# Four sublayers on one core: attention heads rotated in quarters inside the steady loop, and one joint block ahead of the delta rule

## Time and profile before

| | |
|---|---|
| median of 3 runs | 3130.51 us (3123.18 to 3131.16) |
| profiled execution | 3129.02 us, its span 3127.2 us |
| PE busy | 2824.0 us, 90% |
| DVE busy | 1693.7 us, 54% |
| ACT busy | 1081.3 us, 35% |
| POOL busy | 806.9 us, 26% |
| mean granted TensorE clock | 0.947 |

### The profile page before, as it was taken

How to read it: one execution, slowest core, us unless ns; L and a number is a source line. 1 busy time by engine, 2 the same in 40 slices (tenths; PEclk the granted TensorE clock), 3 DMA queues, 4 the chain that set the end, 5 groups by cost and what they waited for, 6 DMA issues and landing times. The chain is left out here.

```text
span 3127.2 us, 38699 instructions
## 1 busy us (share of the span) xinstructions
PE 2824.0 (90%) x13678; PEld 2330.6 (75%) x13678; DVE 1693.7 (54%) x2466; ACT 1081.3 (35%) x1592; POOL 806.9 (26%) x835
## 2 busy tenths in 40 slices
PE   5955888849999999999999749999999878999998
PEld 4754778748888888888888537878888657888887
DVE  4744667564554455444553556666566354465464
ACT  2332433322121111211111317777777612222221
POOL 0006767400000000000000047888878610000000
PEclk8976889969999999999999879999999999999999
DMA  2322222110010000100000030000000001001001
GB/s 81 114 72 54 56 73 57 40 48 21 20 40 20 20 20 20 40 20 20 20 21 0 26 135 24 30 29 28 27 27 28 14 27 41 27 14 40 3 25 41
DMA packets 86058, 114.35 MB, mean 37 GB/s; under 512 B 42512, under 2 KB 62992, under 8 KB 83152
## 3 DMA queue, kind: packets, MB, share of 16 engines
q1 hardware_dynamic: 85968, 113.18, 11.6%
HBM read 86.16 MB, written 26.74 MB: 36 GB/s over the span
## 5 line engine op out<-in xcount | busy, mean ns | idle before, releaser
L1845 POOL TENSOR_TENSOR att_p_lo<-att_probs,att_p_hi 128x768 fp32r<-128x768 f32 x256 | 467.0, 1836 | 120.5 <-ACT att_p_hi L1910 117.1
L1984 DVE TENSOR_REDUCE att_top<-att_q_scores 128x1 f32<-128x1024 f32 x250 | 305.8, 1223 | 223.0 <-PE att_q_scores L2072 215.8
L297 DVE TENSOR_TENSOR fp_hidden<-fp_gelu,fp_up 128x512 f32<-128x512 f32 x128 | 88.0, 688 | 447.6 <-PE fp_up L75 384.8
L1921 ACT ACTIVATE att_probs<-att_k_scores 128x1024 f32<-128x1024 f32 x256 | 262.6, 1026 | 133.9 <-PE att_k_scores L2088 129.9
L1606 POOL MEMSET lat_power<- 128x16 f32 x1 | 0.1, 111 | 1077.8 <-POOLq L52 1077.8
L286 DVE TENSOR_TENSOR k_stream<-k_stream,fp_down 128x512 f32<-128x512 f32 x256 | 175.5, 686 | 91.0 <-PE fp_down L75 87.4
L347 ACT ACTIVATE fp_gelu<-fp_gate 128x512 f32<-128x512 f32 x128 | 76.2, 595 | 421.8 <-PE fp_gate L75 420.8
L2072 PE MATMUL att_q_scores<-att_k_stack,att_q_stack 128*128 128x512 f32 x500 | 189.4, 460 | 28.3 <-DMA att_q_stack<-att_k_stack 14.4
L73 PE MATMUL fp_gate<-f_feat_hi,fp_w_hi 128*128 128x512 f32 x512 | 200.0, 391 | 13.3 <-DVE fp_w_lo L266 13.3
L1910 ACT CAST att_p_hi<-att_probs 128x768 fp32r<-128x768 f32 x256 | 211.5, 826 | 0.0
L74 PE MATMUL fp_gate<-f_feat_lo,fp_w_hi 128*128 128x512 f32 x512 | 199.8, 390 | 0.0
(11 more groups left out here) (343 smaller groups left out, 6502.5 us busy)
## 6 DMA issues: line engine op xcount, KB each, us to landing
f_words<-codes SPq DMA_DIRECT2D x16, 768.0 KB
f_scale<-scales SPq DMA_DIRECT2D x16, 768.0 KB
f_staged<-w_sparse SPq DMA_DIRECT2D x12, 1024.0 KB, 4.8
qkv<-pc_rows SPq DMA_DIRECT2D x9, 1024.0 KB, 4.4
dr_raw<-qkv SPq DMA_DIRECT2D x16, 576.0 KB, 6.2
att_q_stack<-rotated SPq DMA_DIRECT2D x64, 128.0 KB
att_k_stack<-rotated SPq DMA_DIRECT2D x64, 128.0 KB
k_stream<-hidden SPq DMA_DIRECT2D x4, 1024.0 KB, 9.0
```

The lines of the kernel that those rows point to most:

```text
L1845: pool.tensor_tensor(p_lo[:, buffer, :], probs[:, slot, 0:SPLIT], p_hi[:, buffer, :].bitcast(F32), ALU.subtract).then_inc(lo_done, 1)
L1921: act.activation(probs[:, t, :], k_scores[:], ACT.Exp).then_inc(exp_done, 1)
L1984: dve.tensor_reduce(top[buffer][:, STACK + t:STACK + t + 1], scores[:], AX.XY, ALU.max, negate=True).then_inc(max_done, 1)
```

## The change

One function, `project_front`, takes the place of the first block, `normalise`, `project_conv` and `gates_and_decays`. Latent attention prepares only `PREPARED = 2` passes in its prologue; passes 2 to 7 are prepared two passes ahead, a quarter of a pass (256 tokens of a quad) in each head of passes 0 to 5, by `project_piece`, `rotate_piece`, `high_piece`, `low_piece` and `store_piece`, in the bank `turned`. GpSimd's addition goes to VectorE. `passes` has no loop any more. The result `mixed` is written over `values`.

In `project_front`, SP issues: tokens 0, identity, gate weights, tokens 1, gate rows, tokens 2, the first three weight tiles, tokens 3, taps, masks; then the stores and loads of the convolution as before. GpSimd takes the power of four tiles at a time. The transposes and the gates have two PSUM buffers each. The orders of ScalarE, VectorE and TensorE, their helpers left out:

```diff
         @block.scalar
...
+            high(0)
+            act.wait_ge(gate_w_in, 16)
+            act.copy(gate_hi[:], gate_w[:]).then_inc(gate_hi_done, 1)
+            high(1)
+            for i in range(TILES):
+                if i + 2 < TILES:
+                    high(i + 2)
+                gate(i)
+                if i == TILES // 2:
+                    high_weights(0, 0)
+
+            act.preload_act_table_set("natural_log_exp_and_others")
...
+            act.preload_act_table(ACT.Silu)
+
             body(0, True, False)
         @block.vector
...
+            for i in range(SUB):
+                stats(i)
+            moments_of(0)
+            scale(0)
+            scale(1)
+            low(0)
+            dve.wait_ge(gate_hi_done, 1)
+            dve.tensor_tensor(gate_lo[:], gate_w[:], gate_hi[:].bitcast(F32), ALU.subtract).then_inc(gate_lo_done, 1)
+            for i in range(TILES):
+                if i + 2 < TILES:
+                    scale(i + 2)
+                if i:
+                    low(i)
+                if i < 2:
+                    for j in range(2):
+                        stats(SUB + 2 * i + j)
+                elif i + 6 < TILES:
+                    stats(i + 6)
+                if i in (1, 5, 9):
+                    moments_of(i // SUB + 1)
+                if i >= 3:
+                    weight(i - 3)
+                if i == TILES // 2 + 1:
+                    low_weights(0, 0)
+            for i in range(TILES - 3, TILES):
+                weight(i)
...
+        @block.tensor
...
+            turn(0)
+            turn(1)
+            for i in range(TILES):
+                if i + 2 < TILES:
+                    turn(i + 2)
+                gate(i)
```

```diff
         def passes(engine, body):
-            body(0, True, False)
-            with engine.Fori(1, PASSES - 1) as n:
-                body(n, False, False)
-            body(PASSES - 1, False, True)
+            for n in range(PASSES):
+                body(n, n == 0, n == PASSES - 1)
...
+            store_prepared(0)
+            sp.wait_ge(stored[0], 32)
+            for j in range(2):
+                sp.wait_ge(zeroed, 2 * j + 2)
+                load(0, j)
+            store_prepared(1)
             place_top(0)
+            sp.wait_ge(zeroed, 2 * QUAD)
+            for j in range(2, QUAD):
+                load(0, j)
+            sp.wait_ge(stored[1], 32)
             for g in range(HEADS):
+                n, j = divmod(g, QUAD)
                 if g + 1 < HEADS:
                     place_top(g + 1)
+                if has_piece(n):
+                    store_piece(n, j)
+                if n + 1 < PASSES:
                     sp.wait_ge(b_done, T * (g + 1))
+                    if j == 0 and n and not has_piece(n):
+                        wait_stored(sp, QUAD * n - 1)
+                    load(n + 1, j)
...
+            def high_piece(n, j):
+                k = QUAD * n + j
+                act.wait_ge(piece_step, 3 * k + 3)
+                if k:
+                    wait_stored(act, k - 1)
+                act.copy(piece_hi[:], piece[:, 0:PIECE]).then_inc(piece_hi_done, 1)
...
+            def rotate_piece(n, j):          # VectorE, at t == 1, behind the maximum
+                k = QUAD * n + j
+                dve.wait_ge(piece_ps, k + 1)
+                dve.tensor_tensor(piece[:, 0:PIECE], piece[:, 0:PIECE], tables[:, 0, piece_cols(j)], ALU.mult)\
+                   .then_inc(piece_step, 1)
+                if k:
+                    wait_stored(dve, k - 1)
+                dve.tensor_tensor(scaled, piece[:, PIECE:], tables[:, 1, piece_cols(j)], ALU.mult).then_inc(piece_step, 1)
+                dve.wait_ge(piece_step, 3 * k + 2)
+                dve.tensor_tensor(piece[:, 0:PIECE], piece[:, 0:PIECE], scaled, ALU.add).then_inc(piece_step, 1)
+
+            def low_piece(n, j):
+                dve.wait_ge(piece_hi_done, QUAD * n + j + 1)
+                dve.tensor_tensor(piece_lo[:], piece[:, 0:PIECE], piece_hi[:].bitcast(F32),
+                                  ALU.subtract).then_inc(piece_lo_done, 1)
...
+            def project_piece(n, j):
+                b, quad = divmod(n + PREPARED, QUADS)
+                g = QUAD * n + j
+                pe.wait_ge(top_copied, g + 1)
+                if g >= 2:
+                    pe.wait_ge(mixed_done, g - 1)
+                cols = slice(b * SEQ + PIECE * j, b * SEQ + PIECE * (j + 1))
+                for x in range(2):
+                    at = slice(2 * P * quad + x * P, 2 * P * quad + (x + 1) * P)
+                    last = matmul3(pe, piece[:, x * PIECE:(x + 1) * PIECE], wu_hi[:, at], wu_lo[:, at],
+                                   lat_hi[:, cols], lat_lo[:, cols], True, True)
+                last.then_inc(piece_ps, 1)
...
+                if g and has_piece((g - 1) // QUAD):
+                    pe.wait_ge(piece_lo_done, g)
```

More of the change, by code:

```diff
@@ L429, with project_front @@
 N_MASKS = 4
-def project_conv(nc, feat_hi, feat_lo, w_qkv, conv_w, qkv, prefetch):
-    with Scope(nc, "pc") as s:
+def project_front(nc, stream, ident, mask, hidden, ident_in, masks_in, w_qkv, conv_w, w_gate, head_rows, qkv, beta, decay):
+    with Scope(nc, "pf") as s:
+        feat_hi, feat_lo = s.sb("feat_hi", [P, KT, TOKENS], F32R), s.sb("feat_lo", [P, KT, TOKENS], F32R)
+        raw = s.sb("raw_stats", [P, TILES, 6])
+        mean, gap, var, power, rstd = (s.sb(x, [P, TILES]) for x in ("mean", "gap", "var", "power", "rstd"))
+        normed = s.sb("normed", [P, 2, DIM])
+        gate_w, gate_rows = s.sb("gate_w", [P, KT, GATE_COLS]), s.sb("gate_rows", [P, KEY + 2 * HEADS0])
+        gate_hi, gate_lo = s.sb("gate_hi", [P, KT, GATE_COLS], F32R), s.sb("gate_lo", [P, KT, GATE_COLS], F32R)
+        logits, soft = s.sb("logits", [P, TILES, LOGITS]), s.sb("soft", [P, TILES, HEADS0])
+        rate = s.sb("rate", [P, HEADS0])
         taps = s.sb("taps", [P, CT * 3 * CONV])
@@ L468, in _ @@
                 sp.wait_ge(stored[q], 16 * CT + 16)
+            sp.wait_ge(masks_arrived, 16)
         @block.gpsimd
         def _(pool):
+            pool.memset(power[:], -0.5).then_inc(power_done, 1)
             pool.memset(padded[:, :, :, 0:CONV - 1], 0.0).then_inc(zeroed, 1)
+            pool.wait_ge(power_done, 1)
+            for q in range(BLOCKS):
+                at = slice(SUB * q, SUB * (q + 1))
+                pool.wait_ge(moments, 7 * q + 7)
+                pool.tensor_tensor(rstd[:, at], var[:, at], power[:, at], ALU.pow).then_inc(rstd_done, 1)
         @block.scalar
@@ L537, in body @@
                                                      op0=ALU.mult, op1=ALU.add).then_inc(taps_done, 1)
[L539 to L558, removed]
@@ L1513, in _, with delta_attention @@
                 add_output(CHUNKS - 1, b)
[L1517 removed]
+def delta_attention(nc, stream, ident, mask, eye, hidden, ident_in, masks_in, w_qkv, conv_w, w_gate, head_rows, w_out):
     with Scope(nc, "da") as keep:
@@ L2027, in _ @@
             dve.wait_ge(blank_done, 6)
-            for n in range(PASSES):
-                for x in range(2):
-                    multiply(n, x)
-                if n:
-                    low_rotated(n - 1)
-                for t in FIRST_TILES[n]:
-                    maximum(0, 0, t, True, (q_scores, late)[t % 2])
-            low_rotated(PASSES - 1)
+            multiply(0, 0)
+            multiply(0, 1)
+            add_rotated(0)
+            multiply(1, 0)
+            low_rotated(0)
+            multiply(1, 1)
+            add_rotated(1)
+            low_rotated(1)
+            for t in range(T):
+                maximum(0, 0, t, True, (q_scores, late)[t % 2])
             copy_top(0, True)
```

329 lines of the change are left out of this document (175 added, 154 removed).

## The result

| | before | after |
|---|---|---|
| median of the timed runs | 3126.85 us (3120.57 to 3131.16, 4 runs) | 3075.69 us (3071.16 to 3082.31, 4 runs) |
| ratio, 95% interval | | 0.984 (0.9812 to 0.9867) |
| profiled execution | 3129.02 us | 3075.02 us, its span 3073.2 |
| mean granted clock | 0.947 | 0.952 |

What follows compares the result with a forecast made beforehand. TensorE was taken as the limit nearly everywhere, except two troughs, at the start and in attention's prologue. Front -36, prologue -35 and steady part +19 gave -52 from 3129, so 3077 us, range 3060 to 3100.

Steps and rivals of the forecast that it cites:

- a tile: Gate stage interleaved with normalisation: time for each of 16 tiles, taken as 2.8 us, bounds 2.6 and 3.9.
- tail: End of the convolution on VectorE, ScalarE and SP after TensorE's last product: unchanged at 15.4 us.
- Front: Stages ahead of the delta rule: gate tiles moved before the convolution, interleaved with normalisation, -36 us, bounds -28 and -43.
- A: Front: copy, low part and transposes stay in series, 3.9 us a tile, -18 instead of -36, 3095 us; chance 0.10.
- part 3: Steady attention: quarters prepared in 24 heads cost 0.8 us of TensorE each, +19 us, bounds 17 and 34.
- Prologue: Start of latent attention: two prepared passes instead of eight bring the first exponential sooner, -35 us, bounds -40 and -30.
- Steady part: Attention after its prologue: TensorE is full, so six added matmuls a head count in full, +19 us over 24 heads.
- C: Steady attention: weight loads show between a quarter's products, 1.3 us a head, 3089 us; chance 0.06.
- B: Steady attention: VectorE's loop replaces TensorE as the limit, 1.4 to 1.6 us a head, 3092 to 3096 us; chance 0.11.
- count of 0: Steady attention: VectorE's rotation adds nothing, its delay absorbed by the wait at t = 3; bounds 0 and +0.5.
- D: Steady attention: a quarter's store lands late and holds VectorE's next rotation, 3 us in 23 heads, 3146 us; chance 0.03.
- E: Attention's prologue: still held by SP's order, -15 instead of -35, 3097 us; chance 0.06.

Runs made afterwards that it cites:

- front_serial: Changed kernel with the gate stage's order taken back, all 16 tiles transposed before any gate product: ratio 0.9905 to the kernel before, 3096.47 us.
- dve_more: Changed kernel with one more 128x256 multiplication on VectorE in each quarter's rotation, its result unread: ratio 0.9857 to the kernel before, 3081.86 us.
- store_late: Changed kernel with SyncE issuing a quarter's two stores behind the next pass's load instead of ahead of it: ratio 1.038 to the kernel before, 3247.87 us.
- unrolled: Kernel before the change with the attention passes only written out instead of looped: ratio 1.0 to the kernel before, 3130.68 us.

## Why the prediction was right

| step | predicted | measured |
|---|---|---|
| stream of TensorE from | 17.8 us | 16.84 |
| a tile | 2.8 | 2.59 |
| slow TensorE at the start | 2 | 1.5 (first gate 3.67, not 2.2) |
| convolution | 101.6 | 100.4 |
| tail | 15.4 | 15.4 |
| delta rule's first transfer | 181.6 | 176.03 |
| first exponential, in its block | -35 | -34.5 |
| a head | +0.8 | +0.80 |
| 24 heads | +19 | +19.6 |

- **Front.** The mechanism held, at the favourable end of its bounds (-41.6, from -28 to -43). Most of the 5.6 us that I was off lies in the tiles: with their slow start they took 43.2 us (16.84 to 60.0) instead of 46.8. I had put TensorE at 2.7 a tile and VectorE, with its waits for the power, at 2.9, and took 2.8. In the stream the four transposes of a tile hold TensorE for 0.35 us (21.28 to 21.63), not for my 0.56, and the gate for 2.24. VectorE did wait about 1 us for each power, but scalings were two tiles ahead and TensorE never saw that; it waited for VectorE once in this stream, 0.43 us for a low part at 45.3 (A false; front_serial shows what A would have cost, 21 us for my 18). The chain of beta and decay, priced at 6 without cover, was covered.
- **The bounds.** By the sum, 2.6 and 3.9 us a tile give -39 and -18; the -28 and -43 have no working, and -41.6 is beyond the -39. The total's upper bound of 3090 leaves out the unfavourable end of part 3; with all three terms at theirs it is 3105, outside the range.
- **Prologue.** The sum was right with two errors in it. The landing behind the store took 2.66 us, not 4.0; from the load's issue to the first maximum it took 14.3, where my terms give some 12.7; the two nearly cancel. And I took 55 GB/s as given: the largest removable term of that stretch, 7.6 us, was in front of me in the earlier trace rows, and I did not ask why it was a seventh of the 400 GB/s that the 512 KB stores reach in the same trace.
- **Steady part.** TensorE 6 x 0.12 = 0.72 and about 0.08 around it, 0.8 in all. C is false: 0.12 us from product to product with a load each, where the rule that the prediction quotes gives 0.214. The Trainium skill (TensorE: Matmul & The Clock Gate, "The mechanism") names beside that rule a second case in which a weight load runs ahead, the background weight buffer, which the prediction left out; the 0.12 us agree with that case. B did not occur, but dve_more shows that it began at the next operation: the 0.07 us of slack were told rightly, the margin of the count of 0 was nil.
- **D** did not occur (1.8 us to land). Its count of the wait is right to 0.1 us in store_late; its price left out what TensorE loses behind the wait.
- **E** is false: the load is issued 2.66 us behind the store of the low part.
- **Writing out the loop**, nothing: shown by unrolled.
- **The total**, -52 for a measured -54.4 by the traces and -51 by the medians, is closer than its terms, and that part is luck: the front's 5.6 us too little stand against 1.4 between the stages and 0.7 in the attention that I had at nothing.

## What to carry to other kernels

When a stretch waits for transfers, divide bytes by time first: a transfer at a seventh of its neighbours' rate was here a matter of its access pattern, and mending that comes before moving work around it, since the move pays only as long as the transfers are slow. In a chain of engines that wait for each other, test the slack by adding an operation, not only by taking one away. Price a stall of TensorE with the slow products behind it, here 2 us on top of 5.5. And before reading a clock of 1.00, look whether the trace has a record there; the spacing of equal products tells.

## What the runs showed of the hardware

- Transfers whose outermost dimension is 2 ran at 33 to 75 GB/s, and two queues together no faster (51 to 58). A 128 KB store with 128 rows lands in 1.8 us ahead of such a load and in 9.6 behind it, which fits a share of it waiting on the few engines that the load keeps busy.
- The prologue after the change runs at granted clock 0.50, 1.2 GHz, from 1784 to 1802 us, where the earlier trace rows had 0.77 in the longer one. TensorE had been idle for 17.6 us ahead of it. Up to the top row VectorE's maxima stand nearly back to back there, so most of that pace is VectorE's; what the half clock costs in this stretch no run shows.
- The delta rule, with the same instructions, took 428.6 to 436.8 us in the fourteen profiled executions. The granted clock of its first 80 us was 0.61 to 0.69 in all of them, and does not go with the time: 430.1 us at 0.61, 436.4 at 0.69.
